# Splitting the feed-forward weights inside the K/V projection loop, and one fused VectorE step in the ELU

## The reference

```python
x = x + attn_layer(layernorm(x))      # elu/norm linear attention, Wo, LN, FFN (gelu), LN
x = x + bitlinear_ffn(layernorm(x))

# inside attn_layer, B=8, S=2048, H=1024, 16 heads of 64, FF=4096
q, k, v = heads(Wq, bq), heads(Wk, bk), heads(Wv, bv)
eq, ek = elu(q), elu(k)
qn, kn = eq / norm(eq), ek / norm(ek)             # per head
kv  = einsum('bhsd,bhse->bhde', kn, v)
ctx = einsum('bhsd,bhde->bhse', qn, kv) / 8
attn_out = layernorm(ctx @ Wo + bo + x, g1, be1)
h   = gelu(attn_out @ W1 + b1)
out = layernorm(h @ W2 + b2 + attn_out, g2, be2)
```

## Time and profile before

| | us |
|---|---|
| median of 3 runs | 6295.69 |
| lowest, highest | 6254.19, 6420.06 |
| the profiled execution | 6147.8 |
| its span on the slowest core (core 1) | 6146.2 |
| spans of the other cores | 6095.2 to 6141 |
| PE / DVE / ACT / POOL busy on core 1 | 3851.8 / 1574.9 / 1075.9 / 169.1 |

### The profile page before, as it was taken

One profiled execution on the slowest core, in us unless ns is written; L12 is line 12 of the kernel. 1 busy time (PEld: TensorE's weight loads), 2 busy tenths in 40 slices (PEclk: granted clock), 3 DMA queues, 4 the chain that ended last, 5 costly groups with the idle time before them and its releaser, 6 DMA issues.

```text
span 6146.2 us, 49022 instructions; the slowest of 8 cores (6095.2 to 6146.2 us)
## 1 busy us (share of the span) xinstructions
PE 3851.8 (63%) x16008; PEld 1619.7 (26%) x16008; DVE 1574.9 (26%) x1971; ACT 1075.9 (18%) x1151; POOL 169.1 (3%) x228
## 2 busy tenths in 40 slices
PE   1004887574684897798698698400011887869697
PEld 1001333232230342343343343000000332323233
DVE  2443233454203211310310310222223303122220
ACT  2000112231001211211210220222110402213050
POOL 0131000000000000000000000000000000000000
PEclk9998778785796898898898798755555998989899
DMA  2583000000000431331331332022221221222222
GB/s 94 155 231 130 1 1 1 31 1 0 28 0 0 91 95 48 86 93 55 79 94 61 76 93 65 4 72 67 77 65 46 48 62 48 58 52 57 52 55 66
DMA packets 647455, 374.32 MB, mean 61 GB/s; under 512 B 547280, under 2 KB 580256, under 8 KB 646192
## 3 DMA queue, kind: packets, MB, share of 16 engines
q1 hardware_dynamic: 627248, 304.06, 18.7%
q0 software_dynamic: 19968, 67.12, 3.5%
HBM read 312.39 MB, written 58.72 MB: 60 GB/s over the span
## 4 chain that ended last, share of the span: by engine, by line
PE 60%; DVE 14%; DMA 14%; issue 7%; ACT 4%; DVEq 1%; SPq 0%; ACTq 0%; POOLq 0%; POOL 0%
PE ps_h L1163 11%; PE ps_p L1225 11%; PE ps_h L1707 8%; PE ps_y L1786 7%; PE ps_v L490 4%; PE ps_k L490 3%; PE ps_wo L911 3%; DMA ph<-x 2%; PE ps_h L1710 2%; DMA spill_w1p<-phwp 2%; PE ps_q L490 2%; DMA strB<-wfc 2%; DMA spill_w2p<-phwp 2%; DMA spill_pj<-strB 2%; PE ps_s L953 1%
## 5 line engine op out<-in xcount | busy, mean ns | idle before, releaser
L1163 PE MATMUL ps_h<-ph 128*128 128x512 bf16 x3072 | 682.1, 382 | 48.2 <-DVE ph L1125 35.7
L1225 PE MATMUL ps_p<-strB,ph 128*128 128x512 bf16 x3072 | 671.7, 382 | 31.7 <-DMA ph<-spill_w2p 31.7
L1786 PE MATMUL ps_y<-strB,ph8w 128*128 128x512 bf16 x2048 | 470.2, 388 | 71.0 <-DMA ph8w<-spill_pj 56.0
L490 PE MATMUL ps_v<-ph1w,ph1zp 128*128 128x512 bf16 x768 | 225.1, 468 | 431.8 <-DVE ph1zp L480 431.8
L1707 PE MATMUL ps_h<-ph,ph8w 128*128 128x512 bf16 x2048 | 474.2, 386 | 14.3 <-DMA ph8w<-spill_fc 14.3
L1163 PEld LDWEIGHTS ps_h<-ph 128*128 128x128 bf16 x3072 | 296.4, 98 | 433.6 <-issue 97.1
L1225 PEld LDWEIGHTS ps_p<-strB,ph 128*128 128x128 bf16 x3072 | 302.2, 98 | 401.2 <-issue 44.4
L1724 ACT ACT_TABLE_LOAD x128 | 164.2, 1283 | 967.1 <-PE ps_h L1710 939.8
L1179 ACT ACT_TABLE_LOAD x128 | 164.2, 1283 | 732.2 <-PE ps_h L1163 732.2
L1786 PEld LDWEIGHTS ps_y<-strB,ph8w 128*128 128x128 bf16 x2048 | 197.9, 99 | 344.7 <-issue 135.0
L1707 PEld LDWEIGHTS ps_h<-ph,ph8w 128*128 128x128 bf16 x2048 | 192.3, 99 | 331.1 <-issue 125.2
(11 more groups left out here) (207 smaller groups left out, 3560.1 us busy)
## 6 DMA issues: line engine op xcount, KB each, us to landing
ph<-spill_w1p SPq DMA_DIRECT2D x256, 256.0 KB
ph<-spill_w2p SPq DMA_DIRECT2D x256, 256.0 KB
ph8w<-spill_fc SPq DMA_DIRECT2D x128, 256.0 KB
ph8w<-spill_pj SPq DMA_DIRECT2D x128, 256.0 KB
ph<-x SPq DMA_DIRECT2D x32, 512.0 KB
phwp<-w1t SPq DMA_DIRECT2D x32, 512.0 KB
spill_w1p<-phwp POOLq DMA_DIRECT2D x64, 256.0 KB, 4.1
phwp<-w SPq DMA_DIRECT2D x32, 512.0 KB
```

The costliest lines, as they stand in the source:

```text
L490: last = t.matmul(ps[:, cols], zz[:, k * 128:(k + 1) * 128], ww.rearrange("p (k w) -> p k w", k=ND)[:, k, cols], start=(pi == 0 and k == 0 ...
L1163: last = t.matmul(dst, ww[:, k * 128:(k + 1) * 128], aa[:, k, :], start=(pi == 0 and k == 0), stop=(pi == 2 and k == ND - 1))
L1225: last = t.matmul(ps_p2[:, n * 512:(n + 1) * 512], ww[:, n * 128:(n + 1) * 128], mm, start=(i == 0 and pi == 0), stop=False)
L1786: last = t.matmul(ps_y[:, jj * 512:(jj + 1) * 512], buf[:, off + jj * 128:off + (jj + 1) * 128], mm, start=(i == 0 and pi == 0), stop=(i = ...
```

## The change

1. In `elu_norm` and `elu_norm_q` two DVE steps, the addition and the minus 1, become one `scalar_tensor_tensor` that computes (e2 - 1) + e1.
2. The loop of the weight preparation is taken out of its place before the K/V loop and turned into a function `emit_prep_stripe(idx)`. Each K/V iteration calls it four times, after `elu_norm` of its block.
3. Within a stripe the cast to the high half moves from DVE to ACT (`sc.copy`). The subtraction stays on DVE and now waits for ACT. SP's load waits also for ACT's earlier copy of that buffer.
4. The tile `phwp` lives until the end of the K/V stage, and `g_wprep` is taken after the loop.

```diff
@@ elu_norm (and the same in elu_norm_q)
                 b.inc(v.tensor_scalar(e1, blk, 0.0, None, ALU.max), "v", 1)
                 b.wait(v, "v")
-                b.inc(v.tensor_add(e1, e2, e1), "v", 1)
-                b.wait(v, "v")
-                b.inc(v.tensor_scalar(blk, e1, -1.0, None, ALU.add), "v", 1)
+                b.inc(v.scalar_tensor_tensor(blk, e2, -1.0, e1, ALU.add, ALU.add),
+                      "v", 1)
@@ weight preparation
-                for idx in range(2 * NF):
...
-                    def _(v, tb=tb, wpb=wpb, ldv=ldv, gw=g_wp[par]):
-                        b.wait(v, "ld", ldv)
-                        b.wait(v, "gq", gw)
-                        b.wait(v, "v")
-                        b.inc(v.tensor_copy(wpb[:, 0:1024], tb), "v", 1)
-                        b.wait(v, "v")
-                        b.inc(v.tensor_sub(wpb[:, 1024:2048], tb, wpb[:, 0:1024]),
-                              "v", 1)
-                    block.vector(_)
...
+            def emit_prep_stripe(idx):
...
+                def _(sy, tb=tb, src_ap=src_ap, wv_=v_wp[par], ws_=s_wp[par],
+                      idx=idx):
+                    b.wait(sy, "v", wv_)
+                    b.wait(sy, "s", ws_)
...
+                    b.dma(sy, "ld", out=ob, in_=src_ap)
+                block.sync(_)
+                ldv = b.cnt["ld"]
+
+                def _(sc, tb=tb, wpb=wpb, ldv=ldv, gw=g_wp[par]):
+                    b.wait(sc, "ld", ldv)
+                    b.wait(sc, "gq", gw)
+                    b.wait(sc, "s")
+                    b.inc(sc.copy(wpb[:, 0:1024], tb), "s", 1)
+                block.scalar(_)
+                sv = b.cnt["s"]
+                s_wp[par] = sv
+
+                def _(v, tb=tb, wpb=wpb, sv=sv):
+                    b.wait(v, "s", sv)
+                    b.inc(v.tensor_sub(wpb[:, 1024:2048], tb, wpb[:, 0:1024]),
+                          "v", 1)
+                block.vector(_)
...
@@ K/V loop
                     v_elu[si] = elu_norm(kbp_[si % 2])
+                    for pj in range(4):
+                        emit_prep_stripe(si * 4 + pj)
                 emit_kv(NT - 1)
+                g_wprep = b.cnt["gq"]
```

More of the change, by code:

```diff
@@ L500, in build_program @@
              nc.sbuf_tensor("ph1zp", [128, 2048], F32) as ZP:
+            wp_cm = nc.sbuf_tensor("phwp", [128, 4096], F32)
+            WP_scope = wp_cm.__enter__()
             WKVb = WKV[:].bitcast(BF16)
@@ L577, in build_program, with _ @@
-            g_wprep = b.cnt["gq"]
+            WP = WP_scope
+            wp_tmp = [WP[:, 0:1024], WP[:, 1024:2048]]
+            wp_bp = [WP[:, 2048:3072].bitcast(BF16),
+                     WP[:, 3072:4096].bitcast(BF16)]
+            v_wp = [b.cnt["v"], b.cnt["v"]]
+            s_wp = [b.cnt["s"], b.cnt["s"]]
+            t_wp0 = b.cnt["t"]
+            g_wp = [0, 0]
+            def emit_prep_stripe(idx):
+                w2_mode = idx >= NF
+                i = idx % NF
+                par = idx % 2
+                tb = wp_tmp[par]
+                wpb = wp_bp[par]
+                src_ap = (w2_d[i * 128:(i + 1) * 128, :] if w2_mode
+                          else w1t_d[i].transpose([1, 0, 2]))
+                def _(sy, tb=tb, src_ap=src_ap, wv_=v_wp[par], ws_=s_wp[par],
+                      idx=idx):
+                    b.wait(sy, "v", wv_)
+                    b.wait(sy, "s", ws_)
+                    if idx < 2:
+                        b.wait(sy, "t", t_wp0)
+                    ob = tb
+                    if src_ap.ndim == 3:
+                        ob = tb.rearrange("p (k c) -> p k c", k=src_ap.shape[1])
+                    b.dma(sy, "ld", out=ob, in_=src_ap)
[14 more added lines that the diff above has]
+                block.vector(_)
+                vv = b.cnt["v"]
+                v_wp[par] = vv
+                def _(gp, i=i, w2_mode=w2_mode, wpb=wpb, vv=vv):
+                    b.wait(gp, "v", vv)
+                    for hl in range(2):
+                        srcv = wpb[:, hl * 1024:(hl + 1) * 1024]
+                        if w2_mode:
+                            dst = w2p_d[hl, i]
+                        else:
+                            dst = w1p_d[hl, i].transpose([1, 0, 2])
+                            srcv = srcv.rearrange("p (k c) -> p k c", k=ND)
+                        b.dma(gp, "gq", out=dst, in_=srcv)
+                block.gpsimd(_)
+                g_wp[par] = b.cnt["gq"]
@@ L664, in build_program @@
             v_kv = b.cnt["v"]
+            wp_cm.__exit__(None, None, None)
             if phases < 2:
@@ L696, in _ @@
                         b.wait(v, "v")
-                        b.inc(v.tensor_add(q1, q2, q1), "v", 1)
-                        b.wait(v, "v")
-                        b.inc(v.tensor_scalar(blk, q1, -1.0, None, ALU.add), "v", 1)
+                        b.inc(v.scalar_tensor_tensor(blk, q2, -1.0, q1,
+                                                     ALU.add, ALU.add), "v", 1)
                     block.vector(_)
```

## The result

The changed kernel took 6018.23 us in the median of 12 runs (lowest 5892.59), the kernel before 6165.46 us in the median of 15 (lowest 6104.62). In some runs of either kernel the cores of one die run at a lower clock throughout; compared without those runs the ratio is **0.9628, 95% interval 0.9593 to 0.9664**: 3.7% less. The profiled execution went from 6147.8 to 5909.2 us, so 238.6 us less; the sum in the prediction was -235, rounded to -240. Timed again with the last experiment, the changed kernel had a ratio of 0.9674 [0.9601, 0.9746].

What follows compares the result with a forecast made beforehand. Some 285 us of DMA latency in the weight preparation, with PE idle, was taken as the bound. Removing 286.8, less batch and tail costs, gave about -240 from the 6295.7 median: 6055 us, range 5990 to 6130, outer 5940 to 6165.

Steps and rivals of the forecast that it cites:

- the sum: Whole span: -224 us on a high-pace core, -265 on core 1, so about 6146-235 = 5911 us.
- The preparation leaves its place: Before the K/V loop: PE's first K/V matmul starts at 255.1 instead of 541.92, -286.8 us.
- The batch: Four stripes per K/V iteration: 17.9 us (W1), 16.3 (W2); DVE-bound periods add 55 us at high pace, 14 on core 1.
- The tail: End of the K/V stage: the last batch is exposed, Wq's first load comes later, +14 us.
- The fused step: ELU on DVE: one step replaces two, 0.74 to 0.8 us each; PE's waits in the Q stage shrink, -5.6 us.
- the 11.0: K/V loop on DVE: end of L480 to end of L428, 11.8 us less 0.8 for the fused step.
- The later stages: After the Q stage, some 4000 us of mostly PE work: no change forecast.
- the clock takes it back: Rival, later stages: a lower granted clock makes them 3% slower, 120 us return, 6175 us; chance 0.10.
- The batch that fits: Rival, K/V loop: faster writes or copies without table loads end the batch near 13.7 us, 6020 us; chance 0.14.
- Late writes: Rival, K/V batch: landings take twice 4.1 us, batch 26 us, 6175 us, within 2%; chance 0.05.
- PE at its lower clock throughout the loop: Rival, K/V loop: PE runs at 1.2 GHz, period 49.5 us, +230, 6285 us, no change; chance 0.03.
- Slower by the same place: Rival, K/V loop: batches of 40 us, landings near 15, make the kernel 2% slower, 6420 us; chance 0.03.

Runs made afterwards that it cites:

- the last experiment: Changed kernel with two stripes ahead of the ELU and two behind, cast and subtraction on DVE, timed beside the changed kernel: ratio to the kernel before 0.9592.
- the first split: Changed kernel with two stripes' ACT copies before DVE's evacuation, their subtractions after the next split, two stripes behind the ELU: slowest core 5879.8 us, one execution.
- the second split: Changed kernel with two stripes ahead of the ELU, two behind, cast and subtraction on DVE: slowest core 5854.9 us in one execution; ratio to kernel before 0.9592.
- the split kernels: Changed kernel with each batch halved around the ELU, casts on ACT or on DVE: slowest core 5879.8 and 5854.9 us, one execution each.

## Why the prediction was right in its mechanism, and where it was wrong

On core 1 the working held within 11 us in each term. What failed is the last step, the median of three runs to which the difference was applied; it is named below.

**The preparation leaves its place: -286.8.** Right. PE's first K/V matmul starts at 255.08 on core 1, 541.92 before: -286.8.

**The batch: 17.9 us with W1, 16.3 with W2.** The mechanism was right in each step (a table load per copy, write 1 waiting for write 0, copy 3 behind write 1, DVE's queue as the bound), the sizes a little small. Measured on core 7: 18.9, 18.6 and 18.1 for the first W1 batches; 17.3 and 17.1 for two late W2 batches. Over all cores the means are 18.7 for W1 and 17.2 for W2, so each batch was taken 0.8 to 0.9 us too short. For W2 I had let the medians of the earlier trace rows carry more than they could: in a W2 batch on core 7 (at 750.66) POOL waited 4.25 us after both issues for the landing of write 0, where I had reckoned 3.5 from an issue. Periods on core 7: (573.93-294.97)/8 = 34.9 us and (805.44-573.93)/7 = 33.1 us, forecast 34.2 and 32.6. With the tail, the stage from the first matmul to bq grew by 81 us on core 3 (492.96 to 574.15) and by 38 on core 1 (538.6 to 576.5); forecast were 68 and 27. This term was mis-sized by 11 to 13 us: 0.8 to 0.9 us in each of 15 periods is 13.

**The tail: +14.** From the last L427 (805.66) to the first Wq load (829.03) 23.4 us passed, 7.0 before: +16.3.

**The fused step: -5.6 in the Q stage.** 8.7 us in the mean when alone. I had counted only the waits of PE for the scaling step, and these fell as forecast: on core 1 from 20.8 us in 9 places to 15.0 in one, on core 3 from 20.2 to 15.0. Most of the rest is PE's own time for the same 1088 matmuls, 289.2 us before and 284.6 after on core 3, 286.4 and 284.9 on core 1, at a granted clock of 0.72 and 0.73. Why the pace differed stays open. In the K/V loop the step is worth 12.6 us, and that was in the sum, inside the 11.0.

**The later stages.** Forecast: no change. From the first Wo load to the end core 1 took 4574.9 us before and 4567.1 after, core 3 4610.9 and 4570.3, core 7 4588.2 and 4573.9. Nothing was given back, and the granted clock behind the Q stage was the same: on core 1 0.82, 0.87, 0.88, 0.60 and 0.90 in five stretches before, 0.83, 0.88, 0.87, 0.61 and 0.90 in the matching stretches after. So the rival "the clock takes it back" did not occur in this execution. The 40.6 us of core 3 are no gain of the change: before it cores 2 and 3 had taken 19 to 39 us longer there than the others, and no run says why.

**The sum.** Core 1: forecast -265, measured 6146.2-5883.9 = -262.3 = -286.8+37.9-5.5-7.8. Too small a stage term was met by a small gain in the Q and later stages. For the span, -235 was forecast and -238.6 measured, and part of that agreement is luck. The slowest core was core 1 before, held up by the lower pace in 11 of 16 periods of the K/V loop, and core 7 after, held up by the lower pace in the Q stage (505.2 us, some 21 more than cores 0 to 5). Taken for itself core 7 gained 210.5 us and core 3 254.7, where a core at the high pace was to gain 224.

**The step that failed is the last one: the level.** I applied the difference to the median of three runs, 6295.69, although I had written that the profiled execution stood 2.4% below it. Fifteen runs have a median of 6165.46, within 0.3% of the profiled one. Against that level my 6055 us is a forecast of -110 us, 1.8%, and the measured change, 3.7% (some 230 us), is twice that. As a share of its own base the sum said 3.8%, and that was met. On the profiled execution's own time the same sum gives 6147.8-240 = 5908 us, and 5909.2 was measured, so close only with the luck named above. That the measured median, 6018.23, lies near 6055 is luck too: a base taken 130 us too high met a median 109 us above the profiled execution.

**The rivals.** The batch that fits: no, ACT kept its 64 loads and the landings stayed at 4.3 us (core 3, W1); with the casts on DVE they were 4.0, so that the casts leave DVE did not speed the writes. Late writes: no; they land at 5.4 us only with four in flight. PE at its lower clock throughout the loop: no; after 11.20 us of idleness 48 `ps_v` matmuls took 11.99 us, in the kernel before 11.89 to 13.47 after 5.6 us at the high pace (core 1), and `ps_k` took 10.52 in all 16 periods of all cores. Slower by the same place: eight stripes in eight batches cost 117 us and were still no loss.

## What to carry to other kernels

A latency chain that is moved beside other work is not free by having idle engines around it: lay out the whole round trip (load, copy, subtraction, write, landing), compare its length with the window of the queue it is put into, and count what stands behind it in that queue. Where it is too long, cut it in two and put the halves where the round trip of one runs beside other waits; four stripes in one place cost 73 us on a core at the high pace that two and two did not. And apply a difference that was worked out in one execution to that execution's level, not to a median of three runs with a spread of 2.7%.

## What the runs showed of the hardware

- ACT's table loads follow the closures of the program and not the functions: 64 copies in closures of their own took 64 loads of 1283 ns, the same copies in 32 places, half of them behind log and exp, took 16. The Trainium skill says both halves of this: copy is in every set ("ScalarE: Activation LUTs", Table sets: the hidden batching unit), and loads are placed per block ("ScalarE activation tables: per-element evaluation and per-set limits", Table sets in the compiler and the runtime). The traces agree with both together.
- POOL's writes of 256 KB have a median landing of 4.3 us (W1) and 3.1 to 4.0 us (W2) with two in flight, of 5.3 to 5.6 and 5.4 to 5.7 us with four (cores 1, 3 and 7).
- Which cores run a stage at the lower pace changes from execution to execution, of one kernel too: in the K/V loop cores 0 and 1 in the kernel before and in the first split, 6 and 7 in the second split, 2 to 5 in the second execution of that split. In the changed kernel none did in the K/V loop, and cores 6 and 7 took 505 us for the Q stage against 483 to 485 on the others. What chooses them stays open.
- A loop bound by DVE hides the pace; one bound by PE pays for it. In the changed kernel without part 3 cores 4 and 5 ran all 16 periods at the lower pace (below, core 4; one matmul record of the 48 is missing), with bq at 838.7 and 844.1 us, and the six cores at the high pace had 835.5 to 842.6. In the split kernels, which PE bounds, 10 periods at the lower pace cost some 40 us and 15 or 16 cost some 62.

```profile
405.46 12.78 PE L490 MATMUL ps_k<-strB,ph1zp 128*128 128x512 bf16 x47
```
